# A two-layer decoder on one core: the quantised cross product as bfloat16 whole numbers, and two of four streams of a row mixing multiplied on ScalarE

## What is computed

```python
x = _layernorm(x + _L0_attn_ref(x, wq, wk, wv, wo))
x = _layernorm(x + _L0_xattn_ref(x, ctx_4096, x1_scale, x1_zp, x2_scale, x2_zp))
x = _layernorm(x + _L0_ffn_ref(x, W_res, W_pre, W_post, ...))

# _L0_xattn_ref: both operands quantised, then one product per batch
def fake_quant(x, scale, zp):
    q = jnp.clip(jnp.round(x / s + z), 0.0, 255.0)
    return (q - z) * s
return jnp.matmul(fake_quant(x1), fake_quant(x2))     # (2,256,512) @ (2,512,512)

# _L0_ffn_ref: 24 logits per row, 50 rounds of a 4x4 Sinkhorn normalisation, a branch product
H_res = (1.0 - g) * I + g * sinkhorn_log(x_norm @ W_res.T + H_res_base)
y = einsum('btnc,btn->btc', x_streams, H_pre) @ W_branch
x_mixed = einsum('btij,btjc->btic', H_res, x_streams)  # 4 streams of 128 columns
return x_mixed + einsum('btc,btn->btnc', y, H_post)
```

## Time and profile before

| | us |
|---|---|
| median of 3 runs (lowest, highest) | 1461.27 (1459.94, 1463.52) |
| the profiled execution | 1461.67 |
| its span | 1458.6 |
| PE busy in the span | 1407.6 (97%) |
| DVE, ACT, POOL busy | 1075.1, 856.6, 590.2 |
| mean granted TensorE clock | 0.989 of full speed |

### The profile page before, as it was taken

The page is one execution under the profiler, slowest core; times in us unless marked ns, Lnnn a source line. Parts: engine busy times, 40 slices in busy tenths (PEclk is TensorE's granted clock), DMA queues, the critical chain, the costliest instruction groups (busy, mean ns, idle before and its releaser), DMA issues.

```text
span 1458.6 us, 24391 instructions
## 1 busy us (share of the span) xinstructions
PE 1407.6 (97%) x7654; PEld 1179.6 (81%) x7654; DVE 1075.1 (74%) x2492; ACT 856.6 (59%) x2152; POOL 590.2 (40%) x631
## 2 busy tenths in 40 slices
PE   8999999999999989999999999989999999999997
PEld 7888888887788867787778788768888888888875
DVE  5697666687688876766766776667788788877885
ACT  4556555655223147656755755648677677677661
POOL 3555444434022136456555645335243242242221
PEclk9999999999999999999999999999999999999999
DMA  8011110112122341330321321320012012012000
GB/s 324 1 73 73 73 72 4 69 34 102 58 88 88 114 134 57 105 126 30 130 101 42 116 101 58 119 84 30 20 71 85 16 73 87 15 72 78 1 0 29
DMA packets 30133, 107.72 MB, mean 74 GB/s; under 512 B 3847, under 2 KB 13191, under 8 KB 22104
## 3 DMA queue, kind: packets, MB, share of 16 engines
q1 hardware_dynamic: 30040, 106.58, 20.0%
HBM read 97.07 MB, written 9.50 MB: 73 GB/s over the span
## 4 chain that ended last, share of the span: by engine, by line
PE 71%; DVE 13%; issue 6%; ACT 5%; POOL 4%; DMA 1%; ACTq 0%; POOLq 0%; DVEq 0%; SPq 0%
PE bank L192 14%; PE bank L193 13%; PE bank L194 13%; PE bank L1646 7%; PE bank L1816 3%; POOL wq_low L1087 2%; PE bank L324 2%; PE bank L1831 2%; PE bank L347 2%; PE bank L1837 2%; PE bank L1833 2%; PE bank L293 2%; DVE logit L2128 1%; PE bank L1774 1%; PE bank L335 1%
## 5 line engine op out<-in xcount | busy, mean ns | idle before, releaser
L165 POOL TENSOR_TENSOR tmp<-tmp,sin 128x512 f32<-128x512 f32 x80 | 106.9, 1336 | 216.4 <-ACT tmp L150 214.4
L194 PE MATMUL bank<-wo_low,att_high 128*128 128x512 f32 x384 | 150.6, 392 | 0.0
L2128 DVE SCALAR_TENSOR_TENSOR logit<-bank,qss,amask 128x512 f32<-128x512 f32 x128 | 90.9, 747 | 56.8 <-PE bank L194 55.7
L2034 POOL TENSOR_TENSOR qss<-qss,half 128x4 f32<-128x4 f32 x32 | 34.9, 1091 | 200.3 <-DVE qss L2114 200.3
L1646 PE MATMUL bank<-kT,wg 128*128 128x256 f32 x512 | 112.9, 383 | 2.9 <-ACT prob L1680 2.9
L1935 ACT ACTIVATE prob<-logit,rmax 128x512 f32<-128x512 f32 x128 | 91.6, 719 | 37.9 <-DVE rmax L2132 37.9
L1646 PEld LDWEIGHTS bank<-kT,wg 128*128 128x128 f32 x512 | 97.9, 192 | 16.6 <-ACT prob L1680 3.3
L149 ACT ACTIVATE tmp<-bank 64x512 f32<-64x512 f32 x80 | 47.6, 595 | 102.6 <-PE bank L194 96.6
L192 PE MATMUL bank<-l_wo_high,att_high 128*128 128x512 f32 x256 | 104.6, 408 | 1.8 <-DVE att_low L1530 1.1
L193 PE MATMUL bank<-xT_high,wq_low 128*128 128x512 f32 x256 | 102.1, 399 | 0.0
L193 PE MATMUL bank<-l_wo_high,att_low 128*128 128x512 f32 x256 | 99.8, 390 | 0.0
(11 more groups left out here) (290 smaller groups left out, 4392.6 us busy)
## 6 DMA issues: line engine op xcount, KB each, us to landing
wq<-in_l_wq SPq DMA_DIRECT2D x16, 1024.0 KB, 6.6
wo<-in_l_wo SPq DMA_DIRECT2D x16, 1024.0 KB, 4.9
wkv<-in_l_wkv SPq DMA_DIRECT2D x16, 512.0 KB, 5.6
wg<-in_l_wg SPq DMA_DIRECT2D x8, 1024.0 KB, 4.8
wq<-in_x_wq SPq DMA_DIRECT2D x8, 1024.0 KB, 7.3
wo<-in_x_wo SPq DMA_DIRECT2D x8, 1024.0 KB, 4.9
kT<-in_x_wkv SPq DMA_DIRECT2D x8, 512.0 KB, 3.9
kv_keys<-logit SPq DMA_DIRECT2D x8, 512.0 KB, 4.5
```

The costliest lines, as they stand in the source:

```text
L165: eng.tensor_tensor(halves(tmp[4 + j % 2]), halves(tmp[2 + j % 2]), per_batch(sin), ALU.mult).then_inc(sem(f"{l}_sinp"), 1)
L194: return eng.matmul(dst, a_high, b_low, start=False, stop=stop)
L2128: dve.scalar_tensor_tensor(logit[s % 2][:, c, :], bank[3 + c][:, :], qss[p][:, 1, h, 2 * b + c:2 * b + c + 1], amask[:, c, :], ALU.mult, A ...
```

## The change

1. **Quantised product.** Both operands are kept as whole numbers less 128 in bfloat16 (exact). The context needs three operations per tile, not four; its last writes `ctx_int`. For the rows ACT does the scaling and shift on `x` (`cross_affine`), DVE clips and rounds to `row_int`, PE turns that with bfloat16 products (`cross_turn`), ACT copies to `int_T` (`cross_columns`), and PE multiplies in bfloat16.
2. **Zero points.** PE sums the context over its 512 rows (`context_sum_products`, two times four products of 512 columns), behind half of unit 0. ACT and DVE split each sum into two bfloat16 parts, and one more product per row tile adds it with the right factor (`zero_rows`). Four products of 4 columns per tile give the rows' sums, which DVE turns into `row_term`. ACT scales each result out of its bank (`cross_scale`), and DVE adds it, `row_term` and `x` in one instruction. The constants come from `cross_constants`, 13 small DVE instructions, behind the first four context tiles, in group 1.
3. **Order.** The two halves of unit 0 now stand on either side of the cross products. The logits are formed per pair of row tiles (`mix_logits`), the first pair before the second is turned.
4. **Mixing.** ACT multiplies streams 0 and 1 (`mix_streams`, 32 activations on 128x128) behind two of its copies; DVE multiplies 2 and 3 and adds the two products with two 128x512 additions per tile.
5. **Windows.** `KV_WINDOWS` goes from [2, 5, 5, 6, 12] to [3, 5, 5, 6, 11].

```diff
-                        fake_quant(dve, q2[:, t, :], 1, "quant_c", 4 * t)
+                        quantise_context(dve, t)
+                        if t < KC:
+                            cross_constants(dve, t)
...
+        def quantise_context(dve, t):
+
+            src, dst = q2[:, t, :], ctx_int[t // KC][:, t % KC, :]
+            if due(3 * t):
+                dve.wait_ge(sem("quant_c"), 3 * t)
+            dve.tensor_scalar(src, src, quant[:, 5:6], quant[:, 3:4], ALU.mult, ALU.add).then_inc(sem("quant_c"), 1)
+            dve.wait_ge(sem("quant_c"), 3 * t + 1)
+            dve.tensor_scalar(src, src, 0.0, 255.0, ALU.max, ALU.min).then_inc(sem("quant_c"), 1)
+            dve.wait_ge(sem("quant_c"), 3 * t + 2)
+            dve.tensor_scalar(dst, src, ROUND, ROUND + MID, ALU.add, ALU.subtract).then_inc(sem("quant_c"), 1)
...
+        def context_sum_products(pe, b):
+
+            if b == 0:
+                pe.wait_ge(sem("l0_added"), 4 * (NG - 1) + 2)
+                pe.wait_ge(sem("cross_const"), CROSS_CONSTANTS)
+                pe.wait_ge(sem("quant_c"), CONTEXT_QUANTISED)
+            else:
+                pe.wait_ge(sem("att_low"), 8 * NG)
+            for c in range(KC):
+                last = pe.matmul(bank[SUM_BANKS[b]][0:64, :], ones_bf[:, :], ctx_int[b][:, c, :],
+                                 start=(c == 0), stop=(c == KC - 1))
+            last.then_inc(sem("cross"), 1)
+
+        def context_sum_high(act, b):
+            act.wait_ge(sem("cross"), b + 1)
+            act.activation(sum_parts[:, b, :], bank[SUM_BANKS[b]][0:64, :], ACT.Copy).then_inc(sem("cross_scaled"), 1)
+
+        def context_sum_low(dve, b):
+            dve.wait_ge(sem("cross_scaled"), 2 + b + 1)
+            dve.tensor_tensor(sum_parts[32:64, b, :], bank[SUM_BANKS[b]][32:64, :], sum_parts[32:64, b, :],
+                              ALU.subtract).then_inc(sem("quant_c"), 1)
 
         def cross_vector(dve):
             def quantised(t):
-                dve.wait_ge(sem("ln_xT"), t + 1)
-                cols = slice(t * P, (t + 1) * P)
-                fake_quant(dve, (xT[:, :, cols], attT[0][:, :, cols]), 0, "quant_x", 4 * t)
+                dve.wait_ge(sem("cross_scaled"), t + 1 + (B if t >= 2 else 0))
+                dve.tensor_scalar(tmp[t][:, :], tmp[t][:, :], 0.0, 255.0, ALU.max, ALU.min).then_inc(sem("quant_x"), 1)
+                dve.wait_ge(sem("quant_x"), 2 * t + 1)
+                dve.tensor_scalar(row_int[t][:, :], tmp[t][:, :], ROUND, ROUND + MID, ALU.add, ALU.subtract)\
+                   .then_inc(sem("quant_x"), 1)
 
             def add(t):
-                dve.wait_ge(sem("cross"), t + 1)
-                dve.tensor_tensor(x[:, t, :], x[:, t, :], bank[OUT_BANKS[t]][:, :], ALU.add)\
+                dve.wait_ge(sem("cross"), row_summed(t))
+                dve.tensor_scalar(row_term[:, t:t + 1], turn_bank(0, t)[:, 0:1], cs[:, 5:6], cs[:, 6:7],
+                                  ALU.mult, ALU.add).then_inc(sem("quant_x"), 1)
+                dve.wait_ge(sem("quant_x"), 2 * NT + t + 1)
+                dve.wait_ge(sem("cross_scaled"), NT + B + t + 1)
+                dve.scalar_tensor_tensor(x[:, t, :], tmp[t][:, :], row_term[:, t:t + 1], x[:, t, :], ALU.add, ALU.add)\
                    .then_inc(sem("rows_added"), 1)
...
+        def cross_turn(pe, t):
+            pe.wait_ge(sem("quant_x"), 2 * t + 2)
+            for c in range(KC):
+                last = pe.matmul(turn_bank(0, t)[:, c * P:(c + 1) * P], row_int[t][:, c * P:(c + 1) * P],
+                                 identb[:, :], start=True, stop=True)
+            last.then_inc(sem("ln_turn"), 1)
+
         def cross_tensor(pe, t):
-            if t == 0:
-                pe.wait_ge(sem("quant_c"), 4 * B * CT)
-            pe.wait_ge(sem("quant_x"), 4 * (t + 1))
+            cols = slice(t * P, (t + 1) * P)
+            pe.wait_ge(sem("ln_xT"), t + 1)
+            for c in range(KC):
+                last = pe.matmul(turn_bank(0, t)[:, 0:4], int_T[:, c, cols], ones_bf[:, 0:4],
+                                 start=(c == 0), stop=(c == KC - 1))
+            last.then_inc(sem("cross"), 1)
             if t < 2:
                 pe.wait_ge(sem("l0_added"), 4 * (NG - 1) + 3 + t)
             if t == 3:
-                pe.wait_ge(sem("kv_copied"), 1)
+                pe.wait_ge(sem("quant_x"), 2 * NT + 1)
+            dst = bank[CROSS_BANKS[t]]
+            if t == 2:
+                pe.wait_ge(sem("quant_c"), CONTEXT_QUANTISED + 1)
             for c in range(KC):
-                last = pe.matmul(bank[OUT_BANKS[t]][:, :], attT[0][:, c, t * P:(t + 1) * P],
-                                 q2[:, (t // 2) * CT + c, :], start=(c == 0), stop=(c == KC - 1))
-            last.then_inc(sem("cross"), 1)
+                pe.matmul(dst[:, :], int_T[:, c, cols], ctx_int[t // 2][:, c, :], start=(c == 0), stop=False)
+            if t % 2 == 0:
+                pe.wait_ge(sem("quant_c"), CONTEXT_QUANTISED + t // 2 + 1)
+            pe.matmul(dst[:, :], zero_rows[:, :], sum_parts[:, t // 2, :], start=False, stop=True)\
+              .then_inc(sem("cross"), 1)
+
+        def cross_affine(act, t):
+            act.wait_ge(sem("ln_x"), t + 1)
+            act.activation(tmp[t][:, :], x[:, t, :], ACT.Identity, bias=quant[:, 1:2], scale=quant[:, 4:5])\
+               .then_inc(sem("cross_scaled"), 1)
...
+        def cross_scale(act, t):
+            act.wait_ge(sem("cross"), row_summed(t) + 1)
+            act.activation(tmp[t][:, :], bank[CROSS_BANKS[t]][:, :], ACT.Copy, scale=cs[:, 3:4])\
+               .then_inc(sem("cross_scaled"), 1)
+
+        def cross_scalar(act):
+            cross_affine(act, 0)
+            cross_affine(act, 1)
+            for b in range(B):
+                context_sum_high(act, b)
+            cross_columns(act, 0)
+            cross_columns(act, 1)
+            cross_affine(act, 2)
+            cross_affine(act, 3)
+            cross_scale(act, 0)
+            cross_columns(act, 2)
+            cross_columns(act, 3)
+            for t in range(1, NT):
+                cross_scale(act, t)
+            kv_copy(act, 0)
...
+        def mix_streams(act, t):
+
+            if t == 0:
+                act.wait_ge(sem("mix_ready"), 3)
+                act.wait_ge(sem("branch"), NT + 1)
+            for j in range(2):
+                for i in range(STREAMS):
+                    last = act.activation(mixed[j][t][:, i * P:(i + 1) * P], x[:, t, j * P:(j + 1) * P], ACT.Copy,
+                                          scale=hres[:, t, i * 4 + j:i * 4 + j + 1])
+            last.then_inc(sem("branch_part"), 1)
...
-                for j in range(STREAMS):
+                for j in (2, 3):
                     xj = x[:, t, j * P:(j + 1) * P]
                     if j == STREAMS - 1:
                         dve.wait_ge(sem("vector_step"), tally[0])
+                        dve.wait_ge(sem("branch_part"), 2 * NT + t + 1)
+                        for part in mixed:
+                            step(dve, dve.tensor_tensor(acc[:, :], acc[:, :], part[t], ALU.add))
+                        at = [tally[0]] * STREAMS
...
+                    if i == 4 and k in (5, 6):
+                        mix_streams(act, 2 * (k - 5))
+                        mix_streams(act, 2 * (k - 5) + 1)
...
-        KV_WINDOWS = [2, 5, 5, 6, 12]
+        KV_WINDOWS = [3, 5, 5, 6, 11]
...
-                cross_tensor(pe, t)
+            kv_tensor_first(pe, 0, (0,))
+            for b in range(B):
+                context_sum_products(pe, b)
+            for t in range(NT):
+                cross_turn(pe, t)
+                if t % 2:
+                    cross_tensor(pe, t - 1)
+                    cross_tensor(pe, t)
+            kv_tensor_first(pe, 0, (1,))
+            pe.wait_ge(sem("cross_scaled"), 2 * NT + B)
             ln_tensor(pe, 1, 0)
-            kv_tensor_first(pe, 1)
+            kv_tensor_first(pe, 1, (0, 1))
+            mix_logits(pe, 0)
             ln_tensor(pe, 1, 1)
-            mix_tensor(pe)
+            mix_logits(pe, 1)
+            mix_branches(pe)
```

More of the change, by code:

```diff
@@ L230, in decoder_kernel @@
         OUT_BANKS = [3, 4, 1, 0]
+        CROSS_BANKS = [3, 4, 1, 6]
+        MID = 128.0
+        ctx_int = [over("ctx_int0", [P, KC, D], "klow0", dt=BF16), over("ctx_int1", [P, KC, D], "q2", dt=BF16)]
+        sum_parts = over("sum_parts", [64, B, D], "loraB", dt=BF16)
+        row_int = [over(f"row_int{t}", [P, D], f"tmp{4 + t}", dt=BF16) for t in range(NT)]
+        int_T = over("int_T", [P, KC, T], "attT0", dt=BF16)
+        zero_rows = over("zero_rows", [64, P], "zlog", dt=BF16)
+        ones_bf = over("ones_bf", [P, 64], "ztmp", dt=BF16)
+        cs = over("cs", [P, 16], "hres", dt=F32)
+        cs_bf = over("cs_bf", [P, 4], "hres", 64, dt=BF16)
+        row_term = over("row_term", [P, NT], "hres", 96, dt=F32)
         def l0_load_group(sp, g, p):
@@ L1639, in kv_tensor, with kv_unit @@
             groups(nc.tensor, body)
-        def kv_unit(pe, p, n, dst):
```

(7 more changed lines are left out.)

93 lines of the change are left out of this document (62 added, 31 removed).

## The result

| | before | changed |
|---|---|---|
| median of 5 executions | 1461.27 us | 1455.14 us |
| lowest, highest | 1459.93, 1463.52 | 1453.27, 1456.52 |
| profiled execution, its span | 1461.67, 1458.6 | 1456.52, 1454.0 |
| mean granted clock there | 0.989 | 0.987 |

The ratio is 0.9954, with a 95% interval of 0.9941 to 0.9968: faster by 6.1 us, where 7.7 were forecast. The profiled execution is the longest of the changed kernel's five, so between the two profiles the difference is smaller, 5.2 us in time and 4.6 in span. The five executions of the changed kernel spread over 3.3 us, and the shortest have the higher mean clock (1453.27 at 0.990, 1456.52 at 0.987).

The account below looks back on a forecast made before the run. PE, busy for 97% of the 1458.6 us span, was taken as the bound. Cross stage 5.4, context 1.1 and behind the mixing 1.4 sum to 7.9, giving 1453.6 us, range 1450.5 to 1459.5.

Parts of the forecast that it names:

- Cross stage, 5.4: From the cross stage's start to the logits: less PE work, so logits and Sinkhorn rounds come 5.4 us earlier (4.0 to 6.1).
- my floor: Cross stage, products of 4 columns: lowest price assumed, 0.06 us each, with a ceiling of 0.13.
- Context in groups 1 and 6, 1.1: One operation fewer per context tile shortens PE's waits for DVE (1.3 and 1.2 us): 1.1 gained, bounds 0 and 2.0.
- Windows: First border after the branch products: PE's 2.87 us wait near 416 goes, and 1.7 of low clock with it.
- Mixing, 1.9 forecast: Mixing behind the Sinkhorn rounds: streams split between ACT and DVE end DVE's side 1.9 to 2.1 us earlier, counted from S.
- Behind the mixing, 1.4 forecast: From the mixing to layer 1's decay step: 1.4 us gained, between ends of -0.7 and 2.9.
- the row that kept the clock and the row that lost it: PE's idle times behind the mixing: clock kept at 1.52 and 0.83 us, fallen after 2.87; about 1.4 and 1.8 expected.
- the bound of 3.6: Behind the mixing: if the clock falls, the `win` products' 3.59 us double, making that term -0.7.
- The drop of the clock behind the mixing: Rival: clock drops behind the mixing or in the cross stage, costing 3 to 3.6 us; 1457 (1456 to 1458), chance 0.20.
- The slower case: Rival: clock stays low through the whole cross stage, 371 to 390 us; time 1468.3, chance 0.08.
- Three times slower products on ACT: Rival, mixing: ACT's products take 0.8 us each, so the mixing ends some 10 later; 1463.6, chance 0.01.
- The turns: Behind the mixing: taken as plain products with `ident`; if the transpose rule held, the gap would lengthen to 4 us.

Follow-up runs that it names:

- a_twice: The changed kernel with each of the 16 bfloat16 products of the cross stage issued twice; ratio 0.9960, median 1456.1 us.
- a_cross_only: The changed kernel with the mixing back on DVE and the old table of windows; ratio 0.9950, median 1454.9 us.
- b_windows: The kernel before with only the changed table of windows, [3, 5, 5, 6, 11]; ratio 1.0000, median 1462.8 us.
- a_windows_early: The changed kernel with the old table of windows alone, so ACT's stream products stand one copy earlier than in a_windows; ratio 0.9955, median 1455.8 us.
- a_pool_late: The changed kernel with POOL's split of the gate weights moved behind its first sine product; ratio 0.9955, median 1455.9 us.
- a_mix_dve: The changed kernel with all four streams of the mixing back on DVE; ratio 0.9959, median 1455.2 us.
- a_cover: The changed kernel with 33 more products of 128 columns that nobody reads, in PE's idle pieces behind the mixing; ratio 0.9948, median 1455.0 us.
- a_windows: The changed kernel with the old table of windows, ACT's stream products kept behind the same two units; ratio 0.9974, median 1458.4 us.

## Why the prediction was right, and where it was off

- **Cross stage, 5.4: 5.6** (6.83 less the 1.23 by which PE started the stage earlier). The prices of a product (0.23; 20 of them took 5.1, the four with the zero points 0.32 each), of the turns (0.8 to 0.9 for 8, so 0.1 each) and of ACT's copies held. The products of 4 columns cost 0.03 each by the distance of starts, less than my floor; PE's waits in the stage were some 1.2, for 1.7. That PE's work is the path of the stage is shown by `a_twice`, and that parts 1 to 3 carry the gain by `a_cross_only`; how the gain divides between the cheaper product and the new order was not run.
- **Context in groups 1 and 6, 1.1: 1.2.** PE's waits for DVE there, 1.3 and 1.2, became 0.4 and none. The other kernels with the same code start the stage at 364.9 to 366.5, so the size is known to a microsecond only.
- **Windows: mechanism half right.** The branch products ran at full clock, so PE came to the border sooner and waited 2.07 us there, with low clock behind it; I had said that for the last unit this was nearly the same. It ended 109.7 behind S, not 108.1. It did no harm, since DVE's side decided, as forecast, and by the ratios of b_windows and a_windows_early the step is worth nothing. Even this differs from one execution to the next: the same 32 products took 3.82 in eight of the profiles with the new cross stage and between 5.35 and 6.56 in four.
- **Mixing, 1.9 forecast: 0.2** (PE's second turns, behind the last normalisation, start 113.98 behind S for 114.20). This is the term that was mis-sized. A row tile takes 3.74 by DVE, not 3.5, most of the excess in its two additions (1.52 from start to the next group's start, for 1.36), and the first wait was 2.19 for 1.1, because ACT had a unit's copy ahead of its products, began them 0.8 behind DVE, and took 2.4 for the first eight. Where ACT had no copy ahead (a_pool_late) the wait was 1.41 and the second turns started 113.25 behind S, so the term is worth 0.2 to 1.0.
- **Behind the mixing, 1.4 forecast: 1.0 lost.** The step that failed is "the new gaps lie between the row that kept the clock and the row that lost it, and I take 1.4". The clock fell behind 1.39 and 1.82 us of idle time; second turns and `win` products took 2.8 longer, within the bound of 3.6 that I had given. ACT's decay step (L1133 before, L1290 now) started at 124.1 behind S (122.1 before, 119.3 forecast). Of that 2.3 came back, unforeseen: POOL's split ran beside one decay step of DVE, not three, so the scans start 129.1 behind S, for 129.5. The 0.4 went again in the load of the decay rows, and 1.0 at L1642, beside POOL's sine products.
- **Behind M, 1.2 lost**, for which I had no term. In layer 1 the mean clock of 920 to 1000 us was 0.89 for 0.91 before, 1.6 us of full speed in 80. It can't be put down to the change: with the same code there, single profiles lie between 910.0 and 916.1.
- **How much was luck.** The total is in the range because the cross stage and the context, five sixths of the sum, came as forecast. Behind S the forecast had the wrong sign: 1.4 gained was forecast, 1.0 and behind M another 1.2 were lost in the profile. A range of 9 us covered that. That the medians differ by 6.1 and not by 5.2 as the two profiled executions do is the spread of executions.
- **The rivals.** The drop of the clock behind the mixing (chance 0.20) came about at its place, for 2.8 of PE's time where it had 3 to 3.6; the total of 1455.1 lies between the forecast and its 1456 to 1458, since 1.4 of the term was already kept back for it. The slower case never showed: from 370 to 385 us the clock was 1.00 in every profile with the new cross stage, though the pieces are small. From 385 to 395, in logits and branch products, it was 0.66 in a_cross_only and 0.83 in a_mix_dve, a_cover and a_pool_late, as the kernel before had 0.71 at 394. Three times slower products on ACT did not show either (1.27 for four, spaced 1.17: 0.29 each, which is what the Trainium skill, "ScalarE: Activation LUTs", "What ACT_TABLE_LOAD costs", would make of one, by the estimate above).
- **The turns.** The prediction calls them plain products with `ident`. That is wrong: the kernel writes them with `pe.transpose` (L725), and the timeline counts one record for each (x8 for eight), where a float32 product of the same size has two (x30 for the 15 of a_cover). So the rule of the Trainium skill ("TensorE: Matmul & The Clock Gate", "Part 4: PE-mode transpose"), that transposes do not count for the clock gate in the same way, bears on this place and can't be set aside as I did. The runs do not decide on it. For it: the clock stayed at 1.00 in all four kernels whose gaps were filled with plain products. Against it as the whole cause: from the last unit to the second turns PE had transposes and idle time alone for 4.3 us in the changed kernel and in a_twice alike, and only the first lost the clock.

What stays open: why the clock falls behind idle pieces of 1.4 and 1.8 us in the changed kernel and not behind the same pieces in a_twice, 2.4 us later. That they come later is not it: a_pool_late, with the first turns 1.3 earlier than the changed kernel, and a_windows, 4.6 later, have these pieces too and lost the clock. With the pieces filled it stayed up in four profiles of four; unfilled it fell in three of four. How often it falls in the executions that were not profiled is not known.

## What to carry to other kernels

Cut work on the engine that has no gaps, and check with kernels that undo single parts where the gain is: here the first three of five parts together had all of it that could be measured. Where work moves off the full engine, its idle pieces grow, and the clock can take back what was won; a few products that nobody reads kept it up here, and are cheap if they are shorter than the gap. In a program in order, an instruction that waits for another engine's late result must not stand ahead of copies that free the full engine's buffers, nor behind a copy that comes late.

## What the runs showed that I had not expected

- Steps of DVE with two tensor inputs on 32x512 take 0.68 us alone and up to 1.67 beside POOL's 128x512 subtraction; four on 128x128 take 1.13 alone and 2.17, 3.14 or 5.08 by how POOL's work falls beside them. Moving POOL's work moves the loss.
- A kernel with 3.5 us more work on PE's path (a_twice) ended only 1 us later than without; in its profile the clock stayed up behind the mixing.
- The spread of one kernel's executions (3 us) goes with the mean clock, and where the clock falls differs between profiles of the same code (the branch products: 3.82 or 5.35 to 6.56); differences below 1 us between kernels had to be read from the stretches of the trace, not from medians.
